# Fewer counts from TensorE in five gather-and-sum sweeps of a graph network kernel

## The reference

```
edge_index = [src, dst]                          # dst is sorted
# L0: batch norm of x@w1, agg = segment_sum(h[src], dst), gelu(agg@wr + h@wroot), batch norm of (.@w2), + x
# L1: three times: xr = x @ W_rel[l][r] for 8 relations r
#                  agg = segment_sum(xr[edge_type, src], dst);  x = relu(agg + x @ W_root[l] + bias[l])
# L2: red = segment_sum(h[src] + relvec[edge_rel], dst);  x = gru_cell(red, h)
# L3: graph attention: softmax over each node's edges, weighted segment_sum, layer norm, relu
x = layernorm(x + L0(x)); x = layernorm(x + L1(x)); x = layernorm(x + L2(x)); x = layernorm(x + L3(x))
```

## Time and profile before

| what | value |
| --- | --- |
| median of three runs | 9001.03 us |
| span of the profiled execution | 9003.3 us |
| PE busy | 6487.5 us, 72% |
| DVE busy | 4811.1 us, 53% |
| ACT busy | 2496.1 us, 28% |
| POOL busy | 5137.7 us, 57% |
| mean granted TensorE clock | 0.838 of full speed |
| sweeps 1 to 5, from about | 770, 2396, 3640, 4878, 6114 us |
| end of the fifth sweep | 7408 us |

### The profile page before, as it was taken

How to read it: one execution, slowest core, us unless ns; L and a number is a source line. 1 busy time by engine, 2 the same in 40 slices (tenths; PEclk the granted TensorE clock), 3 DMA queues, 4 the chain that set the end, 5 groups by cost and what they waited for, 6 DMA issues and landing times.

```text
span 9003.3 us, 105566 instructions
## 1 busy us (share of the span) xinstructions
PE 6487.5 (72%) x26061; PEld 4172.0 (46%) x26061; DVE 4811.1 (53%) x16511; ACT 2496.1 (28%) x7734; POOL 5137.7 (57%) x5401
## 2 busy tenths in 40 slices
PE   7886777779777877677776555555777776888881
PEld 4443555554345545344444333333444444656661
DVE  5555555545444444343433444443556556887788
ACT  3552111112111111011111222220222224666665
POOL 4555666650266666566665666665666655655550
PEclk9997777879889888788888766776989988999995
DMA  1002333333444445444445666663333335665562
GB/s 50 2 2 63 108 89 91 91 78 133 138 128 134 137 135 131 109 136 135 136 135 148 212 211 207 209 202 104 91 90 92 91 77 163 192 191 187 186 186 72
DMA packets 562316, 1141.95 MB, mean 127 GB/s; under 512 B 115031, under 2 KB 307516, under 8 KB 561598
## 3 DMA queue, kind: packets, MB, share of 16 engines
q0 software_dynamic: 252160, 659.72, 27.5%
q1 hardware_dynamic: 195886, 366.27, 11.5%
q10 hardware_dynamic: 113680, 109.21, 3.6%
HBM read 822.31 MB, written 312.46 MB: 126 GB/s over the span
## 4 chain that ended last, share of the span: by engine, by line
PE 46%; issue 17%; another core or an unknown queue 16%; DVE 13%; ACT 4%; DMA 1%; ACTq 1%; DVEq 1%; SPq 0%; POOL 0%; POOLq 0%
PE ps L1092 16%; PE ps L1307 6%; PE ps L1277 4%; PE ps L1495 4%; DVE AY L1760 2%; PE ps L1482 2%; PE ps L1382 2%; PE ps L1473 1%; PE ps L1468 1%; PE ps L1081 1%; PE ps L1439 1%; DVE AY L2046 1%; PE ps L1440 1%; DVE edges L1623 1%
## 5 line engine op out<-in xcount | busy, mean ns | idle before, releaser
L1760 DVE TENSOR_TENSOR AY<-AY,ps 128x256 f32 (+1 forms) x4160 | 1741.5, 419 | 3179.2 <-PE ps L1092 1564.8
L701 POOL DMA_INDIRECT g<-rel_d,edges x2496 | 2365.5, 948 | 1721.5 <-issue 594.1
L1092 PE MATMUL ps<-g,rows 128*128 128x256 f32 (+1 forms) x4160 | 1378.4, 454 | 333.9 <-DVE AY L1760 128.7
L1092 PE MATMUL ps<-g,oh 128*128 128x256 f32 (+1 forms) x4160 | 1387.3, 451 | 142.1 <-DVE oh L1743 66.3
L1092 PEld LDWEIGHTS ps<-g,rows 128*128 128x128 f32 x4160 | 875.5, 229 | 685.2 <-issue 432.7
L701 POOL DMA_INDIRECT g<-rows_d,edges x832 | 796.5, 957 | 511.7 <-PE ps L1092 217.1
L701 POOL DMA_INDIRECT g<-in_x,edges x832 | 795.8, 956 | 457.5 <-issue 193.7
L1092 PEld LDWEIGHTS ps<-g,oh 128*128 128x128 f32 x4160 | 860.4, 226 | 402.9 <-issue 207.8
L1307 PE MATMUL ps<-AY,turned 128*128 128x512 f32 x1568 | 836.5, 661 | 153.2 <-ACT turned L728 103.4
L2033 DVE TENSOR_REDUCE AY<-ps 128x4 f32<-128x512 f32 x832 | 571.0, 686 | 203.5 <-PE ps L1473 133.1
L728 ACT ACTIVATE wt<-ps 128x512 f32<-128x512 f32 (+1 forms) x448 | 250.0, 559 | 1501.1 <-remote 705.5
(11 more groups left out here) (384 smaller groups left out, 9948.9 us busy)
## 6 DMA issues: line engine op xcount, KB each, us to landing
rel_d<-wt ACTq DMA_DIRECT2D x392, 256.0 KB
turned_d<-AY SPq DMA_DIRECT2D x104, 512.0 KB
wt<-turned_d SPq DMA_DIRECT2D x104, 512.0 KB
AY<-marks_d SPq DMA_DIRECT2D x104, 512.0 KB
rel_d<-g SPq DMA_DIRECT2D x49, 1024.0 KB
g<-rel_d,edges POOLq DMA_INDIRECT x2496
marks_d<-oh SPq DMA_DIRECT2D x104, 256.0 KB
marks_d<-rows SPq DMA_DIRECT2D x104, 256.0 KB
```

The source lines that it names most:

```text
L701: pool.indirect_dma_start(out=g[:, j, 0:width], out_offset=None, in_=table, in_offset=bass.IndirectOffsetOnAxis(ap=edges[:, word, c:c + 1] ...
L1092: pe.matmul(sum_slot(order, j), one_hot_at(j % OHS), g[:, j, 0:width], start=True, stop=True).then_inc(s_mm, 1)
L1760: dve.tensor_tensor(tile_at(A, t, width), tile_at(A, t, width), sum_slot(order, j), ALU.add)\
```

## The change

TensorE adds 1 to `s_mm` only with the last chunk of a group: a group is 2 chunks in the first sweep and 4 in the other four. A function `summed(order, k)` gives the count at which chunk k's whole group is done. GpSimd waits at the first chunk of a group, for the group that lay 16 chunks before, and not at all at the first 16 gathers of the first sweep. VectorE waits at the first addition of a group for the whole group. The one-hot of chunk k waits for the group of chunk k - 8. No instruction that computes or moves data is added, removed or put elsewhere; what every engine does comes in the same order.

```diff
+SUM_GROUP = (2, 4, 4, 4, 4)
...
+SUMS_BEFORE = [sum(NCH // n for n in SUM_GROUP[:k]) for k in range(L1 + 2)]
+
+
+def summed(order, k):
+
+    if k < 0:
+        return summed(order - 1, NCH + k) if order else 0
+    return SUMS_BEFORE[order] + k // SUM_GROUP[order] + 1
...
-            def gathers(word, table, width, free, ahead):
+            def gathers(order, word, table, width):
 
                 for c in range(NCH):
                     j = c % U
-                    pool.wait_ge(free, ahead + c + 1)
+                    if c % SUM_GROUP[order] == 0 and summed(order, c - U):
+                        pool.wait_ge(s_mm, summed(order, c - U))
                     pool.indirect_dma_start(
...
-            gathers(0, a["x"], D, s_mm, 0)
+            gathers(0, 0, a["x"], D)
...
-            pe.sem_inc(s_mm, U)
...
-                pe.matmul(sum_slot(order, j), one_hot_at(j % OHS), g[:, j, 0:width],
-                          start=True, stop=True).then_inc(s_mm, 1)
+                ins = pe.matmul(sum_slot(order, j), one_hot_at(j % OHS), g[:, j, 0:width], start=True, stop=True)
+                if j % SUM_GROUP[order] == SUM_GROUP[order] - 1:
+                    ins.then_inc(s_mm, 1)
...
                 def one_hot(k):
-                    c, j = NCH * order + k, k % U
-                    dve.wait_ge(s_mm, U + c - OHS + 1)
+                    j = k % U
+                    if summed(order, k - OHS):
+                        dve.wait_ge(s_mm, summed(order, k - OHS))
...
-                    if not order or j % 2 == 0:
-                        dve.wait_ge(s_mm, U + c + (2 if order else 1))
+                    if j % SUM_GROUP[order] == 0:
+                        dve.wait_ge(s_mm, summed(order, U * i + j))
```

More of the change, by code:

```diff
@@ L705, in _ @@
             pool.wait_ge(s_prep_dve, PREP_DVE["src"])
-            gathers(0, a["x"], D, s_mm, 0)
+            gathers(0, 0, a["x"], D)
             for b in range(2):
                 pool.wait_ge(s_rel_out[b], 16 * (1 + out_uses[b]))
-            gathers(1, rel_d[0], D, s_mm, NCH)
+            gathers(1, 1, rel_d[0], D)
             for layer in range(1, L1):
@@ L712, in _ @@
                     pool.wait_ge(s_quarter_out[q], 16 * (1 + NT * layer))
-                gathers(1, rel_d[layer % 2], D, s_mm, NCH * (1 + layer))
+                gathers(1 + layer, 1, rel_d[layer % 2], D)
             pool.wait_ge(s_table, 16 * NT)
-            gathers(0, rows_d, D, s_mm, NCH * 4)
+            gathers(L1 + 1, 0, rows_d, D)
             pool.wait_ge(s_att_out, 16 * NT)
```

## The result

The changed kernel takes 9114.78 us (median of 4 runs, 9108.67 to 9121.88) where before, run beside it, takes 8997.95: a ratio of 1.0124, 95% interval 1.0103 to 1.0145. The forecast was 8620 us and its range ended at 9100. The profiled execution's span is 9115.3 us.

A forecast was written before the change was run, and what follows sets the result against it. Late TensorE counts, leaving in line while gathers run, were taken to bound the sweeps; -240 - 95 - 90 + 45 + 0 = -380 us on 9003.3 gave about 8620 us, with an 8-in-10 range of 8120 to 9100.

The forecast's parts named there:

- I take lateness in proportion to the line, as counts leave one by one: In the sweeps, TensorE's counts are late by the number in line; half of 4.98 us a trip saved in sweeps 2 and 3.
- -240: Sweeps 2 and 3: two late TensorE-to-ScalarE handshakes a trip halved, 120 us saved in each sweep.
- -95: Sweep 1: a line 38% shorter saves 2.7 us a trip, the pair wait costs 0.7; 95 us saved.
- -90: Sweep 4: 1.8 us of TensorE's 9.9 idle us a trip saved at ScalarE's wait for transposed one-hots, 90 us.
- +45: Sweeps 2 and 3: VectorE's wait for four leaves TensorE three chunks ahead instead of five; 0.5 us a trip charged.
- Sweep five: The fifth sweep was taken as 0: a shorter line's saving against VectorE's coarser wait on the path.
- -120: Fifth sweep: a line of 9 counts for 21 at two or three handshakes saves 120 us.
- +125: Fifth sweep: VectorE's wait for four delays the bank about 1.5 us and the norm 1.06 us a trip, costing 125 us.
- GpSimd's own coarser wait costs nothing: At GpSimd's gathers: it waits for chunk c - 13 in place of c - 16, then has three gathers free; 0 us.
- A: Rival: the line was the sweeps' only brake, GpSimd runs without stops, some 8100 to 8250 us; gain above 600 us, chance 0.16.
- B: Rival: lateness goes by time, not number; sweep 4 costs +240 us, about 9450 in all; slower, whole or part, chance 0.18.
- What would show it: Signs in the profile after; wrong if ScalarE still starts 3 us behind a quarter's product or sweep 4 grows.

The follow-up runs named there:

- No_gathers_fifth: The changed kernel without the gathers of its fifth sweep, so sums are made of old rows; 8748.5 us in one run.
- plain_loads_fifth: The changed kernel with each fifth-sweep gather replaced by a plain load of 128 other rows lying together; 8756.96 us in one run.
- third group: Runs on one chip of before, changed and two kernels with added GpSimd stops in the fifth sweep; before took 7806.67 us, changed 1.0016 of it.
- before_b: The kernel before, unchanged, run once more for a trace on one chip with the changed kernel; median there 9026.9 us.
- changed_b: The changed kernel once more, on one chip beside before; 9211.98 us, ratio 1.0203.
- fifth_gpsimd_pairs: The changed kernel, but in the fifth sweep TensorE counts pairs and GpSimd waits for a pair, VectorE still for four; 8904.97 us, 0.9892 of before.
- fifth_vector_pairs: The changed kernel, but in the fifth sweep TensorE counts pairs and VectorE waits for a pair, GpSimd still for four; 8991.69 us, 0.9986 of before.
- gpsimd_alone: Before with only GpSimd's waits coarser (two chunks in the first sweep, four in the others), every chunk counted; 9011.51 us, ratio 1.0009.
- first group: Four kernels run on one chip beside before (9000.3 us): three with one part of the change each, one changed with its fifth sweep's waits as before.
- counts_alone: Before with TensorE counting pairs and GpSimd waiting for a pair in sweeps two to five, VectorE's waits as before; 8950.34 us, ratio 0.9938.
- vector_alone: Before with only VectorE's waits coarser (two chunks in the first sweep, four in the others), every chunk counted; 8969.73 us, ratio 0.9966.
- two_pauses_pairs_b: Before with counts and GpSimd waits for pairs in sweeps two to five, plus two GpSimd stops per fifth-sweep trip; 9185.41 us, 1.0171 of before.
- fourth groups: The fourth group: before, changed and two kernels with two added GpSimd stops per fifth-sweep trip, on one chip; before took 9026.9 us, changed 1.0203 of it.
- Fifth_as_before: The changed kernel with the fifth sweep's counts and waits as they were before; 9030.38 us, ratio 1.0034 to before.

## Why the prediction was wrong

- **The reading of the trace before** stands: gathers make TensorE's counts late and a stop of GpSimd lets them pass. No_gathers_fifth and plain_loads_fifth show that the gathers are the cause there; the third group shows that they need something more, which stays unknown. Of the late step-12 handshakes 38 of 39 in before_b, 44 of 45 in changed_b and 44 of 44 in fifth_gpsimd_pairs ended inside a stop, mostly 2 to 3.4 us after the last gather's start. It isn't the whole rule: in fifth_vector_pairs 22 of 45 ended while gathers went on, and in gpsimd_alone 17 of 45.
- **The step that failed** is "I take lateness in proportion to the line, as counts leave one by one". The forecast halved the lateness. ScalarE started 1.83 us after a quarter's product in the mean of sweeps two and three of before_b, and 1.43 us in changed_b. In the first group it was 1.83 us with half of the counts (counts_alone), 1.88 and 1.58 with all of them (vector_alone, gpsimd_alone). So the number of counts in line doesn't set the lateness. Nor did the fifth of it that is gone in changed_b give time: sweeps two and three of changed_b are 17 us longer. Sweeps two to four with counts for pairs (two_pauses_pairs_b) take 3683 us, before_b 3690. What the traces suggest in its place is that GpSimd's stops decide. It runs until it needs a count that is late, at most a ring of 16 row buffers ahead, stops, and the counts pass. In sweeps one to four its time above 1.25 us a gather is 185, 178, 168 and 166 us in before_b, 183, 195, 169 and 166 in changed_b. In the fourth sweep the stops went in number from 91 to 69 and in length, above the 0.30 us of every gap, from 1.70 to 2.32 us. So the terms -240, -95 and -90 came out at +17, -2 and +2, with the +45 for VectorE's shorter lead in the first of these.
- **Sweep five** was put at 0 between -120 and +125 and came at +185. The +125 was looked for at VectorE, at steps 3 and 10; step 12's transposes, which depend on step 10, wait less than before, 161.4 us for 218.6. "GpSimd's own coarser wait costs nothing" was the fault, a term put at nothing: with a wait for pairs instead the sweep is 207 us shorter. The wait sets when GpSimd stops, and so when ScalarE hears of the transposes. The sum also priced each wait by itself, and the table shows that the loss is of the two together.
- **The rivals**: A is out: GpSimd still stops and the kernel is slower. B had the side right (lateness not by number) and its place and price wrong: sweep four, +240, came at +2. A wait for four sums that pass in one stop may cost no more than one for two; no run tests this. That the time fell inside B's branch at all is in part luck, as the loss came from a wait that B didn't price.
- **What would show it** did: with fewer counts in line ScalarE still starts over 3 us behind a quarter's product in 92 of 383 cases in sweeps two and three of changed_b, for 97 of 382 in before_b.

**Left open.** The third group's chip shows no lateness and nothing in the kernels tells why; the first and fourth groups ran on the same chip and still differ by 27 us in before. Changed was 1.0124 in one comparison and 1.0203 in another. From the first to the second it became 97 us slower, nearly all of it outside its fifth sweep (1473 and 1478 us); before became only 29 us slower. So before may have had a longer fifth sweep in the first comparison than the 1294 us of its trace, which was taken with a first gather at 770 us. Fifth_as_before (1379 us where before_b has 1293, in the same code) points at two rhythms of that sweep; no trace of before in a group like the first was taken to show it.

## What to carry to other kernels

Before counts are thinned out, look at what releases the waiters: if several engines are let go within 0.1 us just when a fourth one stops, the stop may carry the news, and fewer messages changed nothing here. An engine with rows to spare can still set the pace by when it stands still; a coarser wait on it moves its stops, and a handshake of two other engines pays. And put a wait for a group where no long side work parts its members.

## What the runs showed of the hardware

- Indexed gathers of GpSimd hold TensorE's semaphore counts back in four of the five groups of runs, by 1.3 to 6 us in the median of the step-12 handshake, and not at all in the third. Plain loads issued by GpSimd, as many bytes, hold none back (0.01 us for 73 counts that fell into one).
- The same kernel took 7807 us on one chip and 9000 to 9028 on others. The granted clock went with it, 0.91 for 0.84, and TensorE idled less: its busy time in the second sweep is 908 us for 936, and the sweep 1062 for 1233.
- After 3.62 us of idle time two matmuls of 128x512 took 2.08 us at a granted clock of 0.50; at full clock the same two took 1.02.
